# Five graph layers on one core: in the 8-head attention pass, other places for the window additions and for TensorE's query products

## What is computed

```python
q = (feats @ Wq.T + bq).reshape(bs, NHEAD, HDIM).transpose(1, 0, 2)
k = (feats @ Wk.T + bk).reshape(bs, NHEAD, HDIM).transpose(1, 0, 2)
v = (feats @ Wv.T + bv).reshape(bs, NHEAD, HDIM).transpose(1, 0, 2)
...
sim = jnp.einsum('hed,hed->eh', qe, ke) * scale
m = jax.ops.segment_max(sim, c, num_segments=bs)
p = jnp.exp(sim - m[c])
s = jax.ops.segment_sum(p, c, num_segments=bs)
attn = p / s[c]
out_e = attn.T[..., None] * ve
...
agg = jax.ops.segment_sum(out_e, c, num_segments=bs)
return agg @ Wo.T + bo
```

## Time and profile before

| | |
|---|---|
| median of 3 runs | 7186.11 us (7186.09 to 7192.34) |
| profiled execution | 7190.02 us, its span 7188.2 us |
| 8-head edge pass | about 1505 to 3216 us of the span |
| busy share of the whole span | PE 65%, DVE 62%, POOL 62%, ACT 38% |
| granted PE clock in the pass | 0.66 to 0.84 of full speed, by stretch of 52 us |

### The profile page before, as it was taken

One profiled execution on the slowest core, in us unless ns is written; L12 is line 12 of the kernel. 1 busy time (PEld: TensorE's weight loads), 2 busy tenths in 40 slices (PEclk: granted clock), 3 DMA queues, 4 the chain that ended last, 5 costly groups with the idle time before them and its releaser, 6 DMA issues.

```text
span 7188.2 us, 103666 instructions
## 1 busy us (share of the span) xinstructions
PE 4639.1 (65%) x17172; PEld 3045.8 (42%) x17173; DVE 4426.1 (62%) x11590; ACT 2761.4 (38%) x6915; POOL 4483.7 (62%) x4928
## 2 busy tenths in 40 slices
PE   3555556867777777767666666747777735555556
PEld 2433334544444444445444444534444423334333
DVE  5555554557777777775566666835556564445456
ACT  0000000546666666654555555545555550000004
POOL 5777775045555555533777777277777737777771
PEclk7777777977877778778777777867777767777776
DMA  3333334366666666655444444344444453333334
GB/s 86 105 105 105 105 105 86 110 196 196 195 199 199 196 194 195 194 141 155 130 133 132 129 130 130 54 142 130 136 131 136 130 130 106 105 105 105 105 104 90
DMA packets 499186, 962.76 MB, mean 134 GB/s; under 512 B 105402, under 2 KB 296509, under 8 KB 491615
## 3 DMA queue, kind: packets, MB, share of 16 engines
q0 software_dynamic: 240064, 696.46, 35.6%
q1 hardware_dynamic: 258749, 262.93, 11.6%
HBM read 895.74 MB, written 64.63 MB: 134 GB/s over the span
## 4 chain that ended last, share of the span: by engine, by line
PE 33%; POOL 19%; issue 19%; DVE 15%; DVEq 6%; DMA 4%; ACT 2%; ACTq 1%; POOLq 0%; SPq 0%
POOL ring L707 19%; PE bank L974 18%; DVE acc L1429 4%; PE bank L1023 3%; DVE acc L1426 2%; DMA ring<-g_t,stage 2%; PE bank L1211 2%; DVE ring L1564 1%; PE bank L1038 1%; PE bank L1039 1%; PE bank L1040 1%; DVE aux L1484 1%; PE bank L1164 1%; DVE ohc L1435 1%; DVEq L1648 1%
## 5 line engine op out<-in xcount | busy, mean ns | idle before, releaser
L974 PE MATMUL bank<-ring,ohc 128*128 128x256 f32 (+3 forms) x8800 | 3159.5, 511 | 1561.5 <-DMA ring<-xs_t,stage 422.8
L974 PEld LDWEIGHTS bank<-ring,ohc 128*128 128x128 f32 x8800 | 2034.5, 249 | 2529.8 <-issue 1013.4
L1429 DVE TENSOR_TENSOR acc<-acc,bank 128x256 f32 (+2 forms) x3520 | 1486.1, 422 | 1476.6 <-PE bank L974 1361.2
L707 POOL DMA_INDIRECT ring<-g_t,stage x1760 | 1733.9, 985 | 521.7 <-issue 466.9
L707 POOL DMA_INDIRECT ring<-kv_t,stage x880 | 885.7, 1006 | 786.4 <-PE bank L974 552.8
L707 POOL DMA_INDIRECT ring<-in_x,stage x880 | 835.5, 949 | 262.4 <-issue 257.3
L707 POOL DMA_INDIRECT ring<-xs_t,stage x880 | 834.0, 948 | 260.8 <-issue 257.4
L837 ACT ACTIVATE aux<-bank 128x512 f32<-128x512 f32 (+1 forms) x26 | 14.9, 572 | 2226.4 <-PE bank L1153 2226.4
L766 ACT ACTIVATE ohc<-iota,rel_c 128x128 f32<-128x128 f32 x1760 | 557.0, 388 | 54.0 <-PE bank L974 53.7
L809 ACT ACTIVATE cl<-cl 128x1 f32<-128x1 f32 (+3 forms) x111 | 22.5, 203 | 1284.8 <-DVE mx L1557 1284.8
L1426 DVE SCALAR_TENSOR_TENSOR acc<-acc,aux,bank 128x264 f32 x880 | 428.3, 487 | 123.4 <-DVE acc L1426 76.1
(11 more groups left out here) (286 smaller groups left out, 5161.2 us busy)
## 6 DMA issues: line engine op xcount, KB each, us to landing
aux<-relb_t SPq DMA_DIRECT2D x56, 1024.0 KB, 5.4
aux<-q_t SPq DMA_DIRECT2D x880, 64.0 KB
relx<-relb_t SPq DMA_DIRECT2D x55, 512.0 KB, 5.1
ring<-g_t,stage POOLq DMA_INDIRECT x1760, 2.8
x<-ring SPq DMA_DIRECT2D x21, 896.0 KB, 4.2
ring<-x SPq DMA_DIRECT2D x21, 896.0 KB, 9.6
mk<-mk SPq DMA_DIRECT2D x445, 32.1 KB
ring<-in_x,stage POOLq DMA_INDIRECT x880, 2.7
```

Of the source, the lines that this page charges most:

```text
L707: g_.indirect_dma_start(out=rings[L][:, slot, 0:W], out_offset=None, in_=table[L][:, :], in_offset=bass.IndirectOffsetOnAxis(ap=stage[:, s ...
L974: return mm(agp[k % AB][:, 0:width], ohc[:, hot, :], rg[:, slot, vo:vo + width], start=True, stop=True)
L1429: tt(win, win, agp[k % AGP[L]][:, 0:width], ALU.add).then_inc(p["added"], 1)
```

## The change

Seven new semaphores (`fwd`, `seen`, `back`, `most`, `lim`, `lim2`, `car`) serve the 8-head pass. On DVE, `ch1`, `ch2` and `ch3` are replaced in that pass by ten functions that wait for each other's semaphores and have no drain. One addition stands between each of them and the next. The additions that stood in pairs between the products and dots stand alone. `turn_scores` waits for the four `dots` directly. The other passes keep `ch1` to `ch3`.

On PE, the offsets of the next batch are loaded after tile 7, into a second set of registers. `turn_scores` comes after window sum 8 (after 11 before), `rows_of` after 9 (after 13 before), `cols_of` after 13 (after 15 before). `dest_rows` r = 0 of the next batch comes after window sum 11, ahead of `cols_of`; r = 1 stays behind window sum 15. Nothing moves on ACT, POOL or SP.

```diff
-                    def load_places(b):
-
-                        pe.load(edos[0:G], blk_r[0:1, ds(b * G, G)])
+                    def load_places(b, par):
+
+                        at_ = 16 * par if L == 1 else 0
+                        pe.load(edos[at_:at_ + G], blk_r[0:1, ds(b * G, G)])
...
-                            at_ = pe.snap(edos[k], min_val=0, max_val=NT - 1) * (2 * AW)
+                            at_ = pe.snap(edos[16 * par + k], min_val=0, max_val=NT - 1) * (2 * AW)
...
                         def turn_scores():
 
                             gate(pe, p["w"], b + (past(L) + 2))
-                            gate(pe, p["s"], b + (past(L) + 1))
                             if L == 1:
+                                gate(pe, p["red"], b * 4 + 4)
                                 tr(m0[0:R, 0:128], sc[:, par, 0:R], ident[:, :]).then_inc(p["st"], 1)
                                 return
+                            gate(pe, p["s"], b + (late(L) + 1))
...
                             if scores:
                                 dest_rows(b, par, 3)
-                            sums_of(4, 12)
+                            sums_of(4, 8)
+                            if feed:
+                                load_places(nb, npar)
+                            sums_of(8, 9)
                             if scores:
                                 turn_scores()
+                            sums_of(9, 10)
+                            if scores:
+                                rows_of()
+                            sums_of(10, 12)
+                            if feed:
+                                dest_rows(nb, npar, 0)
                             sums_of(12, 14)
                             if scores:
-                                rows_of()
+                                cols_of()
                             sums_of(14, 16)
-                            if scores:
-                                cols_of()
                             if feed:
-                                load_places(nb)
-                                dest_rows(nb, npar, 0)
                                 dest_rows(nb, npar, 1)
                             if scores:
                                 turn_back()
...
+                    def scan_forward(b, par, ub):
+
+                        dve.wait_ge(p[f"mk{par}"], ub * (16 * (H + 1)) + (masks(L, par) + 16 * (H + 1)))
+                        dve.wait_ge(p["st"], b + 1)
+                        v.tensor_tensor_scan(out=fw[0:R, :], data0=mk[0:R, par, 0:128], data1=m0[0:R, 0:128],
+                                             initial=-BIG, op0=ALU.add, op1=ALU.max).then_inc(p["fwd"], 1)
+
+                    def scan_backward(b, par):
+
+                        dve.wait_ge(p["fwd"], b + 1)
+                        v.tensor_tensor_scan(out=mx[0:R, ::-1], data0=mk[0:R, par, 1:129][:, ::-1],
+                                             data1=fw[0:R, ::-1], initial=-BIG, op0=ALU.add, op1=ALU.max)\
+                            .then_inc(p["ch1"], 1)
...
+                    def rows_forward(b, par):
+
+                        dve.wait_ge(p["row"], b + 1)
+                        tt(first_rows(0, HW)[:, :, 1:G], per_head(m1[0:1, hd:hd + R])[:, :, 1:G], broken(b, 1, G - 1),
+                           ALU.add)
+                        v.tensor_tensor_scan(out=rows[0:1, 1, 0:HW], data0=srow[0:1, par, 0:HW],
+                                             data1=m1[0:1, tl:tl + HW], initial=-BIG, op0=ALU.add, op1=ALU.max)\
+                            .then_inc(p["seen"], 1)
+
+                    def rows_backward(b, par):
+
+                        dve.wait_ge(p["seen"], b + 1)
+                        v.tensor_tensor_scan(out=rows[0:1, 2, 0:HW][:, ::-1], data0=srow[0:1, par, 1:HW + 1][:, ::-1],
+                                             data1=rows[0:1, 0, 0:HW][:, ::-1], initial=-BIG,
+                                             op0=ALU.add, op1=ALU.max).then_inc(p["back"], 1)
+
+                    def rows_most(b):
+
+                        seen, back = first_rows(1, HW), first_rows(2, HW)
+                        dve.wait_ge(p["back"], b + 1)
+                        tt(first_rows(4, R), seen[:, :, 1:G + 1], back[:, :, 1:G + 1], ALU.max)
+                        tt(first_rows(3, R)[:, :, 0:1], seen[:, :, 0:1], broken(b, 0, 1), ALU.add)\
+                            .then_inc(p["most"], 1)
+
+                    def rows_before(b):
+
+                        most = first_rows(4, R)
+                        dve.wait_ge(p["most"], b + 1)
+                        tt(first_rows(3, R)[:, :, 1:G], most[:, :, 0:G - 1], broken(b, 1, G - 1), ALU.add)\
+                            .then_inc(p["ch2"], 1)
+                        v.tensor_copy(per_head(fprow[0:1, 0, 0:HW])[:, :, 0:1], most[:, :, G - 1:G])
...
+                    def limit_before(b, par):
+
+                        dve.wait_ge(p["col"], b + 1)
+                        v.scalar_tensor_tensor(m2[0:R, :], mk[0:R, par, 129:257], m1[0:R, on - 8:on - 7], mx[0:R, :],
+                                               ALU.add, ALU.max).then_inc(p["lim"], 1)
+
+                    def limit_behind(b, par):
+
+                        dve.wait_ge(p["lim"], b + 1)
+                        v.scalar_tensor_tensor(m2[0:R, :], mk[0:R, par, 257:385], m1[0:R, on - 7:on - 6], m2[0:R, :],
+                                               ALU.add, ALU.max).then_inc(p["lim2"], 1)
+
+                    def carry(b):
+
+                        dve.wait_ge(p["lim2"], b + 1)
+                        tt(cl[0:R, 2:3], m1[0:R, on - 8:on - 7], m2[0:R, 0:1], ALU.subtract).then_inc(p["car"], 1)
+
+                    def differences(b):
+
+                        dve.wait_ge(p["car"], b + 1)
+                        tt(dd[0:R, :], m0[0:R, 0:128], m2[0:R, :], ALU.subtract).then_inc(p["ch3"], 1)
...
                             pair(1)
-                            add(0, 2)
+                            add(0, 1)
                             dots(1)
-                            add(2, 4)
+                            add(1, 2)
                             weigh_four(2)
+                            add(2, 3)
                             pair(2)
-                            add(4, 6)
+                            add(3, 4)
                             dots(2)
-                            add(6, 8)
+                            add(4, 5)
                             pair(3)
-                            add(8, 10)
+                            add(5, 6)
                             dots(3)
+                            add(6, 7)
+                            if scores:
+                                scan_forward(b, par, ub)
+                            add(7, 8)
+                            if scores:
...
+                            add(10, 11)
+                            if scores:
+                                rows_most(b)
+                            add(11, 12)
+                            if scores:
+                                rows_before(b)
+                            add(12, 13)
+                            if scores:
+                                limit_before(b, par)
+                            add(13, 14)
+                            if scores:
+                                limit_behind(b, par)
...
```

25 lines of the change are left out of this document (14 added, 11 removed).

## The result

| | before | after |
|---|---|---|
| median | 7186.1 us | 7000.8 us (6994.95 to 7005.39, 4 runs) |
| ratio to before | | 0.974, 95% interval 0.9724 to 0.9757 |
| profiled execution | 7190.0 us | 6995.0 us, its span 6993.1 us |

The change gains 185 us in the median and 195 us between the two profiled executions. The forecast was 6963 us, from 26.5 us a batch. The first view to read is the busy time over the same 51 batches as in the earlier trace rows, now cut at the ends of L817 after the change (columns as there).

A forecast was written before the change was run, and what follows sets the result against it. No engine is full; a chain of waits bounds the 30.71 us batch. Steps after w (the end of L817) sum to 26.1, taken as 26.5 for the clock; 4.2 x 53 = 223 us off 7186.1 gives 6963, range 6925 to 7090.

The forecast's parts named there:

- rival 3: PE's clock stays low over the query products: 27.2 to 29.3 us a batch, 7000 to 7111 us; chance 0.17.
- rival 1: ACT's `oht` ends the wait, clock mostly up: 25.9 to 27.1 us a batch, 6931 to 6995 us; chance 0.52.
- Rival 2: Waits between DVE's steps cost as much as drains: additions 0.66 us, not 0.41; 27.5 us a batch, 7016 us; chance 0.10.
- The clock: PE's clock back up by 18.7 us after w, so twelve products of r = 0 take 1.35 us.
- The handover from `oht` to PE: `oht` and handover together end at 18.7 us after w, where ACT's `oht` alone takes 18.68 us.
- The additions: On DVE, eight pairs come apart, saving 0.25 us each; an addition alone costs 0.41 us to the next instruction.
- DVE's own chain: DVE has `cols_of` ready at 20.3 us after w, PE gets there at 21.1, so ACT leads by 0.8 us.
- my main step: ACT's `oht` leads: its end releases PE's first product of r = 0, at 18.7 us after w.
- rivals 4 and 6: q rows late: 4, by 1 to 3 us beyond margin, 7015 to 7140, chance 0.07; 6, as in last batch, 7287, 0.05.
- Slower or no effect: Whole kernel: slower, chance 0.05; within 0.2% of 7186 us as new waits eat up the gain, chance 0.04.

The follow-up runs named there:

- warm: Changed kernel plus eight small products that nobody reads behind each of window sums 4 to 8 on PE: 6969.1 us, 0.9688 of before.
- early2: Changed kernel with ACT making `oht` ahead of its last group of `ohc`, on a slower chip: 8369.6 us, 0.98 of before (changed kernel there 0.9803).
- drains_back: Changed kernel with seven `dve.drain()` put back ahead of the row chain's steps, semaphores and additions kept: 7060.2 us, 0.9821 of before.

## Why the prediction was right, and where its terms were off

The time of 7000.8 us lies in the range of 6925 to 7090, 38 us above the forecast. The path was right: the query products behind `oht`, then sum 12, `cols_of` and the limits end last. But two of its terms were too small, and over two thirds of the products the clock did what rival 3 says and not what the forecast says. The band of the forecast itself (rival 1, 6931 to 6995, with 0.52) misses the time by 6 us; the range holds it since it was drawn to take in rivals 2 and 3. The sum by its own steps, in us behind w, for the batch shown above:

| step | forecast | measured |
|---|---|---|
| `oht` ends | 18.68 | 18.68 |
| first product of r = 0 | 18.7 (0.02 on) | 19.18 (0.50 on) |
| sum 12 starts, twelve products | 20.1 (1.35) | 21.34 (2.16) |
| first limit, two sums and `cols_of` | 21.7 (1.6) | 22.97 (1.63) |
| `ch3` ends, three additions between | 24.05 (2.35) | 25.34 (2.37) |
| next w | 26.1 (2.05) | 27.28 (1.94) |

Two terms were mis-sized. They make up 1.3 us, the other steps and the rounding give back 0.1, and the difference of 1.2 us is explained.

- **The clock.** I expected it "back up by 18.7". It came back at about 20.8 (2234.1), and the products took 2.16 us rather than 1.35: +0.81. `warm` shows that this is the cause: with the clock up they take 1.35. The step that failed is the argument from the order. PE has "turning, rows_of and three sums, nearly without a gap" from 13.9 us on, but at the lower level, and this was not enough to bring the clock back by the time I named. What was measured is the low end of rival 3 (27.2 to 29.3 us, 7000 to 7111), to which I gave 0.17. In the changed kernel the clock falls at 2224, after three microseconds in which PE was busy for 0.61, 0.18 and 0.63, and PE is then busy without a gap from 2229.08 on. The Trainium skill, on the page "TensorE: Matmul & The Clock Gate", section "HAM oscillation — how this bites in real kernels", says that waits between bursts throttle PE anew each time; the trace agrees, with 0.50 over eight of the twelve products, and in all 46 batches between 1650 and 2950 us the first and the last product of r = 0 start 2.01 to 2.06 us apart (1.2 with the clock up).
- **The handover from `oht` to PE.** I put it at next to nothing (18.7 with 18.68 for `oht`). In `warm`, where PE is idle and waits, it is 0.47. In the changed kernel the start is 0.50 behind `oht`, and there it has two causes that end together: this handover, and PE's own sums 10 and 11, which run at the lower clock up to the first product (in `early2`, with `oht` 2 us earlier, PE starts at 18.75 or later in 35 of 37 batches). That is +0.48, and removing one of the two alone does not win it. No row stood behind my figure: before the change PE never waited for ACT in the middle of the chain, and L1095 in the earlier trace rows stands behind products. A handover from ACT to an idle PE can be short: L1097 starts 0.14 us behind the end of L812 (2239.47). Between the wait for `oht` and the first product stand two more waits and register work; that these make the difference was not tested.

With `warm` the sum can be closed: 26.1 forecast, plus 0.45 for the handover, is 26.55, and the undisturbed batches take 26.43.

The forecast of a batch was 26.5 and not 26.1, as 0.4 had been added for the clock. A gain of 3.42 us rather than 4.2 over 51 batches costs 40 us. The last two batches gave back 10 of them: I had counted the last at nothing, since q rows made PE wait for 7.85 us in one piece. After the change PE's waits for q rows in the last batches are six, of 0.56 to 2.90 us, 9.0 us in all. That was luck: the forecast had no gain there. The rest (2 us) lies at the two ends: 223 - 40 + 10 + 2 = 195, as measured.

The other points:

- **The additions.** 0.41 us to the next instruction was forecast, 0.40 is measured, and the steps never wait for their semaphores. Rival 2 gives the time that was found (7000 to 7040) and is wrong all the same: its price is not in the rows, and `drains_back` shows what it would have been. The Trainium skill's page "VectorE: DVE Perf Modes", section "The DRAIN you can't avoid", says that the next operation starts only when the pipe is empty, with or without semaphores. But the same paragraph of the Trainium skill says that an operation which is not held starts earlier, and the prediction left that out. The trace is such a case: an addition starts 0.36 and 0.34 us behind the starts of two scans of 0.42 us. An explicit drain adds 0.24 a step.
- **DVE's own chain.** The last numbers for `cols_of` were forecast at 20.3 and stand at 2233.39 + 0.26 - 2213.32 = 20.33. The wait for `rows_of` was to be 1.2 and is 1.50 us. The wait at addition 12 was to be 0.5 to 1.5 and is 1.81, plus 0.25 at the limit, since PE is 1.2 us later.
- **What leads.** I wrote that a first product released by nothing would mean that my main step is wrong. It is released by nothing in this trace, and the step is half right: PE's backlog at the lower level and ACT's `oht` end together. `early2` (PE leads at 18.8) and `warm` (ACT leads at 19.15) show each of the two alone.
- **The q rows (rivals 4 and 6).** In 1650 to 2950 us PE waits for them for 0.7 us in all in the changed kernel, so the copy of destinations did not make them late. (Rival 4's upper end was added up wrongly: 29.5 us a batch gives 7122, not 7140.)
- **Slower or no effect.** Not seen. But DVE's half alone would have been slower (7240.8), through a mechanism that I had not among my rivals: freed DVE time in front of a PE order that doesn't move.

## What to carry to other kernels

Two engines that hand work to and fro may have to be reordered together: spreading additions between the steps gained nothing (1.007 of before) until PE's turns of the scores moved up with them, and more than half of the final gain came only with both. Part of it is the clock: in batches with the clock up in the query products, PE's half alone took 27.1 to 27.4 us, against 27.3 in the changed kernel and 26.4 to 26.5 in `warm`. Where the clock of TensorE is low in the middle of a chain, price its products at the lower level unless a row of the same activity shows otherwise, and see whether unused products ahead of them bring it up (0.9688 against 0.974 here, with forty a batch). When two waits end within half a microsecond of each other, removing one is worth only the difference.

## What the runs showed of the hardware that was not expected

- Products that nobody needs made PE less busy: 957 us of 1300 with 6512 records, 1001 with 4476, since the granted clock went from 0.81 to 0.97.
- PE was busy without a gap from 2229.08 us on and was granted 0.50 until just after 2234, when it got 1.00.
- The same changed kernel takes 7000.8 us on one chip and 8362.6 on another, and it is 0.974 and 0.9803 of the kernel before. On the slower one 23 of 38 batches between 1650 and 2950 us have ACT idle for about 5 us ahead of L815, for a releaser that the records do not name:

```profile
ACT ring L815 <- remote: 119.7, 23, 6.5
```

In the one looked at closely, PE has made `turn_back` (L1098) at 2103.99 us, ACT starts L815 at 2109.23, and from 2106 to 2109 PE, DVE and ACT are all idle. What holds them there stays open.
